# A mixture-of-experts tail reordered: other PSUM banks for the experts' outputs, the first expert's turns among the last block, the routing's links in other places

## The reference, cut to what matters

```python
def _ffn(x, w1, w2):
    h = x @ w1
    x1, x2 = jnp.split(h, 2, axis=-1)
    return x1 * jax.nn.silu(x2) @ w2
capacity = max(1, int(CAPACITY_FACTOR * T / E_r))       # T = 4096, E_r = 7: 585
shared_sum = jax.vmap(_ffn, in_axes=(None, 0, 0))(flat_x, shared_w1, shared_w2).sum(0)
aff = jax.nn.sigmoid(flat_x @ gate_w + expert_bias)
_, topk_idx = jax.lax.top_k(aff, TOP_K)                 # TOP_K = 2
mask = (topk_idx[:, :, None] == jnp.arange(E_r)[None, None, :]).any(axis=1)
score = jnp.where(mask, aff, -1.0).T
_, sel_idx = jax.lax.top_k(score, capacity)             # each expert's 585 tokens
kept = jnp.take_along_axis(mask.T, sel_idx, axis=1)
w = jnp.where(kept, jnp.take_along_axis(aff.T, sel_idx, axis=1), 0.0)
out = jax.vmap(_ffn)(flat_x[sel_idx], routed_w1, routed_w2)
routed_sum = jnp.zeros_like(flat_x).at[sel_idx].add(out * w[:, :, None])
return (shared_sum + routed_sum).reshape(B, S, D)
```

## Time and profile before

| | us |
|---|---|
| median of 3 runs (2039.51 to 2041.14) | 2039.91 |
| the profiled execution, its own time | 2046.15 |
| its span | 2044.3 |
| the last layer, first transpose to last matmul, in that span | 1680.7 to 2034 |

### The profile page before, as it was taken

One profiled execution on the slowest core, in us unless ns is written; L12 is line 12 of the kernel. 1 busy time (PEld: TensorE's weight loads), 2 busy tenths in 40 slices (PEclk: granted clock), 3 DMA queues, 4 the chain that ended last, 5 costly groups with the idle time before them and its releaser, 6 DMA issues. The chain is left out here.

```text
span 2044.3 us, 35178 instructions
## 1 busy us (share of the span) xinstructions
PE 1912.9 (94%) x13798; PEld 1629.1 (80%) x13798; DVE 1396.4 (68%) x2817; ACT 802.7 (39%) x1484; POOL 641.8 (31%) x507
## 2 busy tenths in 40 slices
PE   5799999999999999999999996999989989988997
PEld 3588888888888888999999995776777687767886
DVE  7778888888887866555555552788866847784554
ACT  5545555555455533122222212444534443232332
POOL 2433443333333330000000001776755620002553
PEclk6799999999999999999999997999999978998999
DMA  4211211111222133323223214535443443324774
GB/s 153 87 62 64 73 63 63 63 63 74 73 72 81 46 112 99 110 94 104 89 98 104 93 63 157 183 109 168 146 124 113 134 174 117 124 83 145 179 179 61
DMA packets 111752, 214.66 MB, mean 105 GB/s; under 512 B 14243, under 2 KB 34787, under 8 KB 110563
## 3 DMA queue, kind: packets, MB, share of 16 engines
q1 hardware_dynamic: 104194, 195.30, 28.4%
q0 software_dynamic: 7392, 17.11, 4.1%
HBM read 136.11 MB, written 76.34 MB: 104 GB/s over the span
## 5 line engine op out<-in xcount | busy, mean ns | idle before, releaser
L1415 PE MATMUL psum<-kv,toep 128*128 128x288 f32 x1280 | 328.3, 419 | 40.5 <-ACT yx L1463 24.3
L1415 PEld LDWEIGHTS psum<-kv,toep 128*128 128x128 f32 x1280 | 249.3, 196 | 117.0 <-ACT yx L1463 30.4
L168 PE MATMUL psum<-xn_t_h,w_gate_h 128*128 128x256 f32 x768 | 232.9, 303 | 1.3 <-DVE xn_th L293 1.3
L168 PE MATMUL psum<-xn_t_h,w_up_h 128*128 128x256 f32 x768 | 217.6, 283 | 0.0
L169 PE MATMUL psum<-xn_t_l,w_up_h 128*128 128x256 f32 x768 | 217.5, 283 | 0.0
L170 PE MATMUL psum<-xn_t_h,w_gate_l 128*128 128x256 f32 x768 | 217.5, 283 | 0.0
L169 PE MATMUL psum<-xn_t_l,w_gate_h 128*128 128x256 f32 x768 | 217.3, 283 | 0.0
L170 PE MATMUL psum<-xn_t_h,w_up_l 128*128 128x256 f32 x768 | 216.7, 282 | 0.0
L161 POOL TENSOR_TENSOR rstd<-rstd,minus_half 128x2 f32<-128x2 f32 x48 | 35.2, 733 | 520.3 <-DVE rstd L157 520.3
L276 ACT ACTIVATE xn_th<-psum 128x256 f32<-128x256 f32 x192 | 73.8, 384 | 312.1 <-PE psum L170 311.0
L1077 POOL TENSOR_SCALAR_AFFINE_SELECT operands<-operands 128x512 f32<-128x512 f32 x128 | 93.9, 733 | 320.9 <-ACT operands L820 320.9
(11 more groups left out here) (313 smaller groups left out, 4820.0 us busy)
## 6 DMA issues: line engine op xcount, KB each, us to landing
toep<-ssm_padded_scratch SPq DMA_DIRECT2D x64, 256.0 KB, 3.5
kx<-in_ctx_pairs SPq DMA_DIRECT2D x32, 384.0 KB, 4.4
x_scratch<-x_all SPq DMA_DIRECT2D x21, 512.0 KB, 2.8
x_all<-in_x SPq DMA_DIRECT2D x16, 512.0 KB, 3.8
operands<-in_ctx_t SPq DMA_DIRECT2D x16, 512.0 KB, 4.9
xn_t_scratch<-xn_t_h SPq DMA_DIRECT2D x16, 512.0 KB, 2.7
xn_t_scratch<-xn_t_l SPq DMA_DIRECT2D x16, 512.0 KB, 3.6
xn_t_h<-xn_t_scratch SPq DMA_DIRECT2D x16, 512.0 KB, 3.7
```

What stands on the lines that cost most here:

```text
L168: pe.run.matmul(out, lhs[0], rhs[0], start=first, stop=False)
L1415: ins = pe.run.matmul(out, w[:, (o - k) * P:(o - k + 1) * P], pairs, start=(k == 0), stop=(k == o))
```

## The change

Three edits, all of them to the tables that set order and banks. No instruction is added or dropped.

1. `routed(e, i)` uses banks 6, 7, 2, 3, 6 instead of 6, 7, 6, 7, 6. Banks 2 and 3 hold the second column tile of the hidden layer.
2. Expert 0's `slot_turn` 0 and 1 stand behind parts 4 and 5 of the last block, 2 behind its last part, ahead of the last `hidden_low`, and 3 and 4 behind that.
3. The links are spread otherwise. Each block but the first takes up nine links instead of eight: one stands inside the four `out` steps, around the third. A `count` that would follow a block half's `product` stands ahead of it; the `hidden_low` behind it comes one part later, behind that part's `count`. Empty links are put in, and `place` stands one part further from `choose`.

```diff
--- before.py
+++ after.py
@@ -1784,13 +1784,17 @@
 
 
 
+
+
             links = [([("affinity", 1), ("rank", SEEN // 8)], []), ([("mask",)], [])]
-            links += [([], [])] * 6 + [([], [("score_turn",)])]
+            links += [([], [])] * 6 + [([], [("score_turn",)]), ([], [])]
             links += [([("count", i)], [("total", i)]) for i in range(len(BITS))]
-            links += [([("final",)], [("final_total",)]), ([("choose",)], [("place",)]), ([("number",)], [("slots_turn",)]),
-                      ([("slots",)], [])]
+            links += [([("final",)], [("final_total",)]), ([("choose",)], []), ([], [("place",)]),
+                      ([("number",)], [("slots_turn",)]), ([("slots",)], []), ([], [])]
             for c in range(2 * TOKT // HOT):
                 links.append(([("hot", c)], [("table", c - 1)] if c else []))
+                if c in (2, 5):
+                    links.append(([], []))
             links.append(([], [("table", 2 * TOKT // HOT - 1)]))
             links.append(([("ids",)] + [("gather", e, i) for e in range(2) for i in range(NT)], []))
             links = iter(links)
@@ -1806,6 +1810,7 @@
                 order.append(("split", j))
             order += [("rank", c) for c in range(SEEN // 8)]
 
+            before_part, after_part = next(links)
             for blk in range(NBLK):
                 later = []
                 if 0 < blk < NBLK - 1:
@@ -1813,17 +1818,34 @@
                 more = [("weights", 1, i) for i in range(PIECES)] if blk == NBLK - 2 else []
                 for part in range(8):
                     f, half_, piece = part // 4, 1 - part // 2 % 2, part % 2
-                    before_part, after_part = next(links, ([], []))
+                    if part % 4 == 0:
+                        low_made = (blk or part) and before_part and before_part[0][0] != "count"
+                        if low_made:
+                            order.append(("hidden_low", blk, 0) if part else ("hidden_low", blk - 1, 1))
+                    elif part % 4 == 1 and (blk or part > 1) and not low_made and before_part and before_part[0][0] != "count":
+                        order.append(("hidden_low", blk, 0) if part > 1 else ("hidden_low", blk - 1, 1))
+                        low_made = True
                     order += before_part
-                    if part % 4 == 0 and (blk or part):
-                        order.append(("hidden_low", blk, 0) if part else ("hidden_low", blk - 1, 1))
+                    if part % 4 == 1 and (blk or part > 1) and not low_made:
+                        order.append(("hidden_low", blk, 0) if part > 1 else ("hidden_low", blk - 1, 1))
                     order.append(("hidden", blk, f, half_, piece))
                     order += after_part
+                    before_part, after_part = next(links, ([], []))
+                    if part % 4 == 3 and before_part and before_part[0][0] == "count":
+                        order += before_part
+                        before_part = []
+                    if blk == NBLK - 1 and part in (4, 5):
+                        order.append(("slot_turn", 0, part - 4))
                     if part % 4 == 3:
                         order.append(("product", blk, f))
                     if part == 1 and blk:
                         for j in range(BLK):
+                            if j == 2:
+                                order += before_part
                             order.append(("out", blk - 1, j))
+                            if j == 2:
+                                order += after_part
+                                before_part, after_part = next(links, ([], []))
                             if j:
                                 order.append(("out_add", blk - 1, j - 1))
                             order += later[j:j + 1]
@@ -1831,8 +1853,7 @@
                         order.append(("out_add", blk - 1, BLK - 1))
                     if part >= 8 - len(more):
                         order.append(more[part - 8 + len(more)])
-            order.append(("hidden_low", NBLK - 1, 1))
-            order += [("slot_turn", 0, i) for i in range(NT)]
+            order += [("slot_turn", 0, 2), ("hidden_low", NBLK - 1, 1), ("slot_turn", 0, 3), ("slot_turn", 0, 4)]
             for j in range(BLK):
                 order.append(("out", NBLK - 1, j))
                 if j:
@@ -1867,7 +1888,7 @@
                 elif name in ("out", "slot_turn"):
                     banks.plan((name, *at), 4 + at[1] % 2)
                 elif name == "routed":
-                    banks.plan((name, *at), 6 + at[1] % 2)
+                    banks.plan((name, *at), (6, 7, 2, 3, 6)[at[1]])
 
             def piece_of(n, i):
                 if i < KT:
```

## The result

The changed kernel took 2031.23 us, the median of 5 runs (2030.69 to 2035.89), against 2039.91 before (5 runs, 2039.51 to 2041.14). The ratio is 0.996, 95% interval 0.9946 to 0.9975: 8.7 us less by the medians, faster by more than 0.2%, but 0.2 us outside the range of the forecast and well short of its 14.9 us. The mean of the three ratios is 0.9946, 11 us.

The account below looks back on a forecast made before the run. TensorE was taken to set the pace, so only its idle or lower-clock time could be gained. 8.4 + 3.6 + 0.8 + 0.8 + 0.8 + 0.5 = 14.9 us took the median from 2039.9 to 2025.0, range 2021 to 2031.

Parts of the forecast that it names:

- term 3: Search's first turn: first count's wait 0.95 us shorter, net gain 0.8, plus 0.8 for half a lower-clock spell.
- term 4: Blocks 1 to 3, counts ahead of products: 2.2 us of waits go, 1.35 come; net gain 0.8, between 0 and 2.
- term 5: End of the search to the table: 10.6 us lost becomes 9.6; gain taken as 0.5, between -2.5 and +2.5.
- term 2: Hand-over to the first expert: outputs start 4.45 us behind the last part, not 7.54; gain 3.6, between 3.1 and 4.8.
- term 1: Experts' outputs: third tile in bank 2 no longer waits for VectorE's eviction; six stalls of 1.41 us, gain 8.4.
- The step from the profile to the median: Profiled execution 6.2 us above the runs' median; the whole gain was carried over, so the median goes from 2039.9 to 2025.0.
- no gather was late: Rival: expert 0's gathers land 3 us later, TensorE waits 2 us at the first turn; 2028 us, chance 0.12.
- The crowding rival: Search's end to table: evictions behind a hot cost 2 us each and bring two spells; 2030.5 us, chance 0.12.
- The clock stayed at 1.00 through the experts: Rival: outputs over four banks bring 1.2 GHz at times between 1871 and 2026 us, making the kernel slower; chance 0.03.
- those of being right: No expert eviction waits, experts 22.1 us apart, block 7's outputs 4.5 us behind its last part, about 2.2 at final_total.
- One of being wrong: The stretch from the search's end to the table taking over 51 us would show the forecast wrong.

Follow-up runs that it names:

- e1_banks: The kernel before with the first edit alone (third output tile in bank 2, fourth in 3, fifth in 6): 2034.0 us against 2041.66, ratio 0.996.
- e5_fill: The changed kernel plus 21 matmuls with unread results, filling TensorE's pauses at final_total and the hand-over: 2029.77 us against 2043.38 for the kernel before, ratio 0.9924.
- e10_before: The kernel before, unchanged, measured against itself: ratio 0.9999, single runs from 2037.77 to 2050.68 us.
- e2_turns: The kernel before with the second edit alone (first expert's turns 0 and 1 inside the last block, 2 ahead of the last hidden_low): 2040.17 us, ratio 0.9991.
- e4_again: The changed kernel once more, unchanged, beside the kernel before: 2028.77 us against 2041.66, ratio 0.9936.
- e11_third: The changed kernel a third time, unchanged, beside the kernel before: 2030.95 us against 2043.37, ratio 0.9943.
- e8_evict: The changed kernel with hot 0 and hot 7 one eviction later: 2032.67 us against 2043.38 for the kernel before, ratio 0.9946.
- e6_bank6: The changed kernel with the first expert's fifth turn in bank 6: 2027.91 us, ratio 0.9923 to the kernel before.
- e7_final: The changed kernel with block 4's first product and low part moved behind choose and place: 2029.32 us against 2043.38 for the kernel before, ratio 0.9935.

## Why the prediction was wrong

The direction, the waits and most of the places were right. The sum was too high by 3 us against the layer's profiles and by 4 against the mean of the three ratios, and the first comparison lies another 2 us below that mean. Mean lengths of the layer's stretches, over profiles whose order in the stretch is that of before or that of the change (us; 4 profiles of each order in every row, but 6 of the new at the hand-over; gains are taken before rounding):

| stretch | before | changed | gain | forecast |
|---|---|---|---|---|
| first transpose to outputs 1 (term 3, part of 4) | 57.1 | 55.8 | 1.4 | 1.6 and more |
| outputs 1 to 3 (term 4) | 36.9 | 36.3 | 0.6 | 0.8 with the part above |
| outputs 3 to 6 (term 5) | 66.0 | 67.6 | -1.5 | +0.5 |
| outputs 6 to first expert (term 2) | 29.4 | 26.5 | 3.0 | 3.6 |
| first to seventh expert (term 1) | 141.0 | 132.5 | 8.5 | 8.4 |
| sum | | | 11.9 | 14.9 |

**Term 1** was right in mechanism and size, also alone (e1_banks), with `hidden_low` 1.8 us early as said.

**Term 5 is the term that failed most.** Its waits came nearly as walked, 9.5 us together if 0.16 is added to each of the six as the prediction does, against 9.6: at `final_total` 2.06 (forecast 2.2), at the outputs of block 4 0.96 and 1.51 (1.0 and 1.8), at a table 1.35 (0.2 and 1.1 at two), at block 5 1.56 and 1.11 (1.7 and 1.5). What was left out is what such a wait brings. The step says of the clock only that before had lost a spell of 1.7 there, and adds none for the new wait of 2.2 us at `final_total`. It brought a spell in six profiles of six, 1.3 us (e5_fill), while the spell that I took as lost before is there in only two of four profiles (e10_before and e2_turns have none). That moves the term by about 2 us, from +0.5 to -1.5. The executions without a spell tell the waits from the clock: 65.2 us from outputs 3 to 6 in the old order (e10_before, e2_turns), 66.2 in the new (e5_fill). The new waits alone lose 1.0 us, so the forecast gain of this term hung on the old spell that it counted as won. (The stretch of the earlier trace rows has seven stalls, not eight; that is 0.16 us.)

**Term 2**: the waits of 1.8 and 1.1 us were 1.89 and 1.11, and the outputs began 4.79 us behind the last part instead of 4.45. The clock behind them differs from execution to execution, before (28.3 to 29.8 us) and after (25.1 to 27.7), so that 3.0 us is the mean of a gain between 0.6 and 4.7. In the first profile of the change the lower clock cost 2.4 us (7.97 - 5.6), where 1.2 was taken, but in e4_again and e11_third it cost nothing, and there the outputs began 4.53 us behind the last part. On the mean of the six profiles it cost 1.2 us, as forecast, if e2_turns is taken without its wait for a gather. Most of what is missing lies on the other side: the forecast started from an execution with 29.8 us, and the mean of the four is 29.4.

**Term 3**: the first wait was 2.40 us, 0.93 less, as worked out. But the lower clock behind it stayed in all six profiles with that wait (19.6 us from the first outputs to the next; 18.2 in the three where the wait was 1.50 us or less), so the 0.8 us for it was not earned. The first profile of the change and e8_evict:

```profile
1718.93:1738.50 19.57, 19.42 (x81) 15.16 (x82) 14.74 (x47) 3.68 (x8) 0.00 (x0) 0.91 0.31 108
```

```profile
1717.48:1735.73 18.25, 18.05 (x81) 14.04 (x82) 14.53 (x47) 3.69 (x8) 0.00 (x0) 1.00 0.34 115
```

**Term 4**: the 0.21 us waits went; each block's first output waits 0.15 to 0.16 us for `hidden_l` (0.25 lost was forecast). Right.

**The step from the profile to the median** failed too. The prediction says: "none of the terms lies in that difference" (the 6.2 us between the profiled execution and the median). Part of it did. A second profile of the same kernel has a last layer 3.7 us shorter, 2.9 of it by lower clock in two stretches whose waits differ by 0.13 us at most. I had read the spells of one execution as if every execution had them, and three terms (2, 3 and 5) counted some of them as a gain.

**The rivals**: no gather was late in the changed kernel: TensorE shows no wait at the first two turns. (In e2_turns one was, by 0.75 us.) The crowding rival (evictions behind a hot, more lower clock, 2030.5) was the nearest to what happened: the clock came, the waits were no longer than walked. The clock stayed at 1.00 through the experts.

**The signs**: those of being right all showed. One of being wrong can't be used: from the fourth `total` from the end to the last table it is 57.2 us, over the 51 named, but with the links moved TensorE has 248 matmuls in that piece and not 219, so its length says nothing. Outputs 3 to 6 hold the same matmuls in both orders but for two tiny ones of the search.

**How far the cause is settled.** That the three edits give 8.5, 3.0 and 0.4 us in the layer, 11.9 in all, rests on profiles, and agrees with the mean ratio of 11 us. Why the first comparison gave 8.7 and the two others 12.9 and 12.4 us is not: its interval reaches from 5.1 to 11.0 us, and single executions of one program scatter by 10 us and more, of which the layer's own spells explain some 4 and the moment at which it starts up to 12. What moves that moment was not tried. The traces show where it arises: by about the 400th matmul, some 75 us into the span, the thirteen profiles are 5.0 us apart; they stay so to 1229 us; the rest is added between there and the layer.

## What to carry to other kernels

Where one engine paces the kernel, look at what stands ahead of a bank's eviction in another engine's stream. Here four subtractions stood there, and giving the later tiles banks whose readers must be through anyway was worth 1.4 us per expert and was the one edit whose value could be read off one profile to 0.1 us. Price a new wait of TensorE with the lower clock that may follow, and don't book the lower clock of one execution as a loss of the kernel: read a second profile first. Before a wait is taken away, look for the next dependence behind it: in e6_bank6 and e8_evict most or all of the wait came back there, while in e7_final, which put the awaited short chain ahead of longer work, 1.4 us of waits and a spell of 1.3 went.

## What the runs showed of the hardware

A wait of 2.0 to 2.1 us of TensorE was followed by lower clock in some executions of a program and not in others. The wait of 2.04 us at `place` before the change brought a spell in two profiles of four; the one of 2.06 us at `final_total` in six of six; the pair of 1.89 and 1.11 us at the hand-over gave stretches at a mean clock of 0.88, 0.94 and 1.00. When the pause at `final_total` was filled with matmuls whose result nobody reads, the one profile of it has no spell. The Trainium skill (TensorE: Matmul & The Clock Gate, "HAM oscillation — how this bites in real kernels") warns only of gaps longer than these; the runs here show that a shorter one, of 2.06 us, can be enough.

Single executions of the unchanged kernel ran from 2036.37 to 2050.68 us, and the point at which its last layer began moved by up to 12 us between profiles of programs that are alike up to there.
